# Expert results of a routed layer: plain scatters and two loads against adding scatters and one load

## The chip, the cores and the metric

One core of one Trainium2 chip runs the whole program. The metric is the device time of one execution in microseconds (us), the median of three runs.

## The reference, cut to what matters

Two layers work on 16 x 256 = 4096 tokens of 128 features, in fp32. Each layer has a mixing part (a scan in the first, an attention with relative positions in the second) and a feed-forward part with 8 experts, of which each token uses two. The change touches only the second layer's feed-forward part and what follows it:

```python
logits = relu(x @ Wr1 + br1) @ Wr2 + br2          # 8 experts
p = softmax(logits); (p1, e1), (p2, e2) = top_2(p)
w1, w2 = softmax over the pair, temperature 2      # b_ex = exp((p2 - p1) / 2), w1 = 1/(1 + b_ex), w2 = b_ex/(1 + b_ex)
shared = silu(x @ Ws1 + bs1) @ Ws2 + bs2
expert[e](x) = silu(x @ We1[e] + be1[e]) @ We2[e] + be2[e]
out = X + gate * (shared + w1 * expert[e1](x) + w2 * expert[e2](x))
```

The pair's weights are written here as the kernel computes them; x is the normed and modulated row of a token, X the residual row, gate a vector for each batch entry.

## The kernel before, in words

Tokens lie in 8 chunks of 512 (4 rows of each of 128 partitions, TPC = 4). The block after the attention is written out by hand for each engine. Routing goes in four groups of two chunks: `choose(g)` (lines 1493 to 1513, VectorE) finds the two experts of a token, `destinations(g)` (1515 to 1525) the two slots, and GpSimd scatters each token's row twice, with 64 indirect DMAs (line 741), into `dispatched_rows`, an area in DRAM where each expert has its rows together. A row is 128 features and one number, the place where the result has to go (RW = D + 1). Rows that no token fills come from a padding table that SP (SyncE) copied there early (lines 468 to 479).

Then 39 tiles (NG) of 256 rows run, each of one expert. Tile j uses slot k = j mod 4 of the buffers (UT = 4). The order of the queues for one tile is:

- SP, `next_tiles` (620 to 628): waits until tile j - 4 has left the slot (`s_ys`), loads the 256 rows (line 598) and the expert's weights, 578 KB (line 604).
- TensorE, in the order `up_tile(j)` (2142 to 2151), `transpose_tile(j + 1)` (2135 to 2140), `down_tile(j - 1)` (2153 to 2161).
- ScalarE, `hidden` (984 to 990): four Silu activations.
- VectorE, `tile_in(j + 1)` then `results(j - 1)` (1607 to 1620). `tile_in` waits for the transposes and for `s_yo[k]`, the landing of tile j - 4's scatters, because it overwrites their index column `rid` (line 1613); it then copies the transposed rows (1615). `results` adds the bias into `YS` (1619) and increments `s_ys`.
- GpSimd, `results_out` (745 to 751): waits for `s_ys` only, then issues two indirect DMAs (line 749), each 128 rows of 128 floats, to `expert_results`, where each token has two rows, one for each of its experts. Their landing is counted in `s_yo[k]`. Scatters of different tiles never meet in a row and may be under way together.

The end (the tail): once all scatters have landed SP loads both rows of every token, 16 loads of 256 KB (line 634). For each chunk ScalarE scales the first row by w1 (1004), VectorE adds w2 times the second (1645) and adds the gated sum into X (`add_gated`, lines 1127 and 1130), and SP stores the chunk (639). The weights of all tokens are worked out once, by VectorE and ScalarE (1598 to 1605, 982).

`link(...)` makes VectorE wait for its own instruction before the next one that reads its result.

Of the kernel before, what the change touches and what calls it, by code (L numbers as in the profile page):

```python
# [23 lines left out]
P = 128  # L24
# [11 lines left out]
E = 8  # L36
# [26 lines left out]
RW = D + 1  # L63
# [7 lines left out]
PADR = (E + SPARE) * GT  # L71


def build(nc, A, out):
    ctx = ExitStack()
    with ctx:
# [149 lines left out]
        rowid = R.take(2 * NT).rearrange("p (k t) -> p k t", k=2)  # L226
# [16 lines left out]
        b_m1, b_m2, b_w1, b_w2 = [R.take(NT) for _ in range(4)]  # L243
# [10 lines left out]
        YG = [v.rearrange("p t n -> p (t n)")[:, 0:NT * D].rearrange("p (t n) -> p t n", t=NT) for v in ROWS]  # L254
# [25 lines left out]
        yD = scratch("expert_results", [2 * TOK + PADR, D])  # L280
# [108 lines left out]
        s_xt = sem("s_xt")  # L389
        s_ys = sem("s_ys")  # L390
# [3 lines left out]
        s_y1 = sem("s_y1")  # L394
        s_fin = sem("s_fin")

# [34 lines left out]
        def _(sp):  # L431
# [149 lines left out]
            for dst, src in ((Wr1[:, :], A["wr1"]), (Wr2[0:33, :], A["wr2"]), (br1[0:32, :], A["br1"]),  # L581
                             (iota1[:, :], A["iota"]), (rowid[:, :, :], A["rowid"]), (steps[:, :, :], A["steps"]),
                             (below[:, :], A["below"]), (restart[:, :], A["restart"]), (reach[:, :, :], A["reach"]),
                             (woT1[:, :], A["woT1"]), (W1S[:, :], A["w1s"])):
                sp.dma_start(dst, src).then_inc(s_wm[1], 16)
# [46 lines left out]
            for c in range(NC):  # L632
                for k in range(2):
                    sp.dma_start(YG[k][:, c * TPC:(c + 1) * TPC, :],
                                 yD[k * TOK:(k + 1) * TOK, :].rearrange("(p t) d -> p t d", p=P)
                                 [:, c * TPC:(c + 1) * TPC, :]).then_inc(s_yl[c], 16)
            for c in range(NC):
                sp.wait_ge(s_fin, c + 1)
                sp.dma_start(out[c * CH:(c + 1) * CH, :].rearrange("(t p) d -> p t d", p=P),
                             X[:, c * TPC:(c + 1) * TPC, :]).then_inc(s_out, 16)  # L640
# [4 lines left out]
        def _(pool):  # L645
# [86 lines left out]
            pool.wait_ge(s_pad, 16 * (E + 1))  # L732
# [20 lines left out]
            with pool.Fori(0, FULL) as i:  # L753
                for k in range(UT):
                    results_out(i * UT + k, k)
            for k in range(LAST):
                results_out(FULL * UT + k, k)
# [3 lines left out]
        def _(act):  # L761
# [188 lines left out]
            values_out(NP - 1, (0, 1))  # L950
            features(3)
# [10 lines left out]
            rows_out(4)  # L962
            relative_out(NP - 1, (1, 2))
# [7 lines left out]
            for c in range(3):  # L971
                shared_hidden(c)
# [6 lines left out]
            for c in range(4, NC):  # L979
                shared_hidden(c)  # L980
            act.wait_ge(s_lg, GROUPS + 2)
            nc.scalar.activation(b_w2[:, :], b_m2[:, :], ACT.Exp).then_inc(s_el, 1)
# [16 lines left out]
            act.wait_ge(s_lg, GROUPS + 3)  # L999
            for c in range(NC):  # L1000
                act.wait_ge(s_yl[c], 32)
                for t in range(TPC):
                    T = c * TPC + t
                    ins = nc.scalar.activation(YG[0][:, T, :], YG[0][:, T, :], ACT.Copy, scale=b_w1[:, T:T + 1])
                ins.then_inc(s_y1, 1)
# [3 lines left out]
        def _(dve):  # L1009
# [424 lines left out]
            def ids(lo, hi):  # L1434
                for k in range(2):
                    ins = v.tensor_copy(ROWS[k][:, lo:hi, D:RW], rowid[:, k, lo:hi].unsqueeze(2))
                ins.then_inc(s_ids, 1)
# [55 lines left out]
            def choose(g):  # L1493
# [13 lines left out]
                link(best_of(b_CD[:, :, :], b_m2[:, ts], b_OH2[:, :, :]))  # L1507
                link(v.tensor_tensor(ME[:, :, :].rearrange("p e t -> p t e"), b_OH1[:, :, :], b_OH2[:, :, :], ALU.add))
# [89 lines left out]
            link(v.tensor_tensor(b_m2[:, :], b_m2[:, :], b_m1[:, :], ALU.subtract))  # L1598
            v.tensor_scalar(b_m2[:, :], b_m2[:, :], 0.5, None, ALU.mult).then_inc(s_lg, 1)
            for c in range(4, NC):  # L1600
                shared_out(c)
            dve.wait_ge(s_el, GROUPS + 2)
            link(v.tensor_scalar(b_w1[:, :], b_w2[:, :], 1.0, None, ALU.add))
            link(v.reciprocal(b_w1[:, :], b_w1[:, :]))
            v.tensor_tensor(b_w2[:, :], b_w2[:, :], b_w1[:, :], ALU.mult).then_inc(s_lg, 1)

            def tile_in(j, k):
# [5 lines left out]
                v.tensor_copy(rid[:, k, :].unsqueeze(2), XR[:, k, :, D:RW])  # L1613
# [27 lines left out]
            for c in range(NC):  # L1641
# [545 lines left out]
def constants():  # L2187
# [6 lines left out]
    k["rowid"] = np.stack([place, place + np.float32(TOK)], axis=1)  # L2194
    count = np.arange(64, dtype=np.float32)
    k["steps"] = np.tile(np.stack([count, count * np.float32(GT)])[None], (P, 1, 1))
    k["padding"] = np.zeros((PADR, RW), dtype=np.float32)
    k["padding"][:, D] = 2 * TOK + np.arange(PADR)
# [98 lines left out]
```

## Time and profile of the kernel before

| what | value |
|---|---|
| median of 3 runs | 961.08 us (956.97 to 962.22) |
| the profiled execution, first to last instruction | 1008.9 us |
| TensorE busy in it | 838.6 us (83%) |
| VectorE / ScalarE / GpSimd busy | 592.7 / 371.3 / 255.6 us |
| DMA | 108.37 MB, mean 107 GB/s |
| mean granted TensorE clock | 0.890 |

All durations below are from the profiled execution. The profile gives its span, 1008.9 us, and no other time of it; that is 47.8 us above the median of the unprofiled runs. In its rows a time is in us from the span's start; PE is TensorE, PEld its weight loads, DVE is VectorE, ACT ScalarE, POOL GpSimd, SP SyncE and SPq what SyncE's queue issues; "out<-in" names what an instruction writes and reads. A number in brackets behind a row is how long the engine had been idle before it, and behind the arrow stands what ended that.

### The profile page before, as it was taken

To read this page: it belongs to the slowest core of one execution; us is meant where nothing else is said; L and a number is where in the kernel's file an instruction comes from. 1 tells how busy PE (TensorE), PEld (TensorE's weight loads), DVE (VectorE), ACT (ScalarE), POOL (GpSimd) and SP (SyncE) were. 2 spreads that over 40 slices of the span, in tenths; PEclk is the share of its full clock that TensorE was granted. 3 is DMA by queue.
4 is the path that set the end of the run, shared out by engine and by line. 5 is a ranking of instruction groups with operands and counts; after the bars stand their busy time and mean duration, and the time that the engine had idled before them with its cause. 6 is when DMAs were issued, how large, how long until landed. Compare 5 with 4: busy or idle time off the path is not lost.

```text
span 1008.9 us, 22593 instructions
## 1 busy us (share of the span) xinstructions
PE 838.6 (83%) x8710; PEld 572.5 (57%) x8710; DVE 592.7 (59%) x1638; ACT 371.3 (37%) x719; POOL 255.6 (25%) x252
## 2 busy tenths in 40 slices
PE   5545698999958789999999999986679789999960
PEld 3443365656634446656656656553257578888850
DVE  8632866666688787687687687763245232222217
ACT  3335221222214105435435436553325324444424
POOL 0522000000073601012011112034661514444440
PEclk9956699999989958999999999997688779999985
DMA  5600022226414761133233332121310417777746
GB/s 147 268 3 0 1 92 92 92 92 211 140 49 140 233 174 48 29 95 89 46 94 60 74 94 62 31 59 34 86 41 9 131 55 213 212 220 215 212 130 223
DMA packets 107827, 108.37 MB, mean 107 GB/s; under 512 B 48892, under 2 KB 93644, under 8 KB 106796
## 3 DMA queue, kind: packets, MB, share of 16 engines
q1 hardware_dynamic: 103196, 97.82, 33.7%
q0 software_dynamic: 4544, 9.35, 2.6%
q8 instruction: 60, 0.98, 0.4%
q14 instruction: 27, 0.22, 0.1%
HBM read 82.15 MB, written 44.78 MB: 126 GB/s over the span
## 4 chain that ended last, share of the span: by engine, by line
PE 62%; DVE 18%; issue 7%; ACT 5%; POOL 3%; DMA 3%; SPq 2%; POOLq 0%; DVEq 0%; ACTq 0%
PE bank L2148 8%; PE bank L2158 7%; PE bank L1928 7%; PE bank L1762 5%; PE bank L1773 5%; PE bank L1774 4%; PE bank L1868 4%; DVE sb_arena L1360 4%; PE bank L2077 3%; PE bank L1820 3%; PE bank L2067 3%; PE bank L1846 3%; DVE sb_ST L1023 2%; DVE sb_arena L1350 2%; DVE sb_arena L1352 2%
## 5 line engine op out<-in xcount | busy, mean ns | idle before, releaser
L1360 DVE TRANSPOSE_TENSOR_REDUCE sb_arena<-bank 128x16 f32<-128x512 f32 x192 | 120.3, 685 | 25.4 <-PE bank L1868 24.2
L901 ACT ACTIVATE sb_arena<-bank 128x512 f32<-128x512 f32 x192 | 99.2, 602 | 50.0 <-PE bank L1868 50.0
L989 ACT ACTIVATE sb_arena<-bank,sb_arena 128x256 f32<-128x256 f32 x156 | 65.3, 471 | 99.9 <-PE bank L2148 99.1
L749 POOL DMA_INDIRECT expert_results<-sb_arena x78 | 74.7, 958 | 105.5 <-DVE sb_arena L1619 88.9
L1762 PEld LDWEIGHTS bank<-sb_arena 128*128 128x128 f32 x512 | 67.9, 195 | 42.1 <-issue 25.3
L858 ACT ACTIVATE sb_arena<-bank 128x512 f32<-128x512 f32 x64 | 38.2, 597 | 143.9 <-PE bank L1774 143.8
L2148 PE MATMUL bank<-sb_arena 128*128 128x256 f32 x312 | 80.3, 402 | 3.8 <-DVE sb_arena L1615 1.8
L1928 PE MATMUL bank<-sb_arena 128*16 128x128 f32 x1024 | 71.9, 422 | 9.5 <-issue 9.4
L1762 PE MATMUL bank<-sb_arena 128*128 128x128 f32 x512 | 70.2, 281 | 10.5 <-DVE sb_arena L1192 10.5
L741 POOL DMA_INDIRECT dispatched_rows<-sb_arena x64 | 63.0, 984 | 62.7 <-DVE sb_arena L1525 44.4
L2158 PE MATMUL bank<-sb_arena 128*128 128x128 f32 x624 | 75.9, 275 | 0.0
L1254 DVE SCALAR_TENSOR_TENSOR sb_arena<-bank,sb_arena 128x128 f32<-128x128 f32 x256 | 71.7, 343 | 2.0 <-PE bank L1762 2.0
L2158 PEld LDWEIGHTS bank<-sb_arena 128*128 128x128 f32 x624 | 72.8, 192 | 0.1
L1192 DVE TENSOR_TENSOR sb_arena<-sb_arena,bank 128x512 f32<-128x512 f32 x64 | 43.7, 685 | 49.6 <-ACT sb_arena L858 49.0
L1773 PE MATMUL bank<-sb_arena 128*128 128x512 f32 x128 | 69.0, 622 | 0.0
L1774 PE MATMUL bank<-sb_arena 128*128 128x512 f32 x128 | 67.5, 609 | 0.0
L2148 PEld LDWEIGHTS bank<-sb_arena 128*128 128x128 f32 x312 | 58.3, 197 | 15.5 <-issue 5.3
L1820 PE MATMUL bank<-sb_arena 128*128 128x56 bf16 (+1 forms) x512 | 62.2, 281 | 5.5 <-DVE sb_arena L1340 3.2
L1350 DVE CAST sb_arena<-bank 128x512 bf16<-128x512 f32 x64 | 43.7, 682 | 37.0 <-PE bank L1820 37.0
L1613 DVE CAST sb_arena<-sb_arena 128x2 uint32<-128x2 f32 x39 | 7.8, 200 | 97.9 <-DMA expert_results<-sb_arena 81.3
L1868 PE MATMUL bank<-sb_arena,sb_identb 128*32 128x128 bf16 (+1 forms) x2304 | 63.1, 242 | 0.4 <-DVE sb_arena L1350 0.4
L1846 PE MATMUL bank<-sb_arena 32*128 32x256 bf16 x512 | 52.9, 285 | 6.8 <-DVE sb_arena L1360 4.5
(263 smaller groups left out, 1356.5 us busy)
## 6 DMA issues: line engine op xcount, KB each, us to landing
sb_arena<-in_w SPq DMA_DIRECT2D x39, 578.0 KB
dispatched_rows<-in_padding SPq DMA_DIRECT2D x8, 2064.0 KB, 9.5
sb_arena<-dispatched_rows SPq DMA_DIRECT2D x39, 129.0 KB
sb_arena<-q_parts SPq DMA_DIRECT2D x8, 512.0 KB, 5.5
sb_arena<-k_parts SPq DMA_DIRECT2D x8, 512.0 KB, 7.0
context_rel<-sb_arena SPq DMA_DIRECT2D x256, 8.0 KB
sb_arena<-expert_results SPq DMA_DIRECT2D x16, 256.0 KB, 5.9
q_parts<-sb_arena SPq DMA_DIRECT2D x24, 128.0 KB, 2.4
```

Of the source, the lines that this page charges most:

```text
L749: nc.gpsimd.indirect_dma_start(yD[:, :], bass.IndirectOffsetOnAxis(ap=rid[:, k, r:r + 1], axis=0), YS[:, k, r, :], None).then_inc(s_yo[k], 16)
L901: nc.scalar.activation(dst, src, ACT.Exp).then_inc(s_ex, 1)
L1360: v.tensor_reduce(dst.rearrange("p h b -> p (h b)"), bank[r % RING][:, :].rearrange("p (b c) -> p b c", c=32), AX, ALU.max, apply_transpos ...
L1762: ins = mm(bank[4 + j % 2][:, t * D:(t + 1) * D], HM0[:, j % 2, t * P:(t + 1) * P], W0[:, k, 2 * F0:3 * F0], start=True, stop=True)
L1773: mm(bank[j % 2][:, :], W0[:, k, 0:F0], chunk(hT, c), start=True, stop=True)
L1774: mm(bank[2 + j % 2][:, :], W0[:, k, F0:2 * F0], chunk(hT, c), start=True, stop=True).then_inc(s_up[0], 1)
L1820: ins = mm(out[:, :, :, x], GT4[:, first:first + 32, :].rearrange("p x a -> p (x a)"), queries[:, :, :, q], start=True, stop=True, skip_gr ...
L1846: mm(dst[:, x * S:(x + 1) * S], KG[k][rows, g, 0:P], QG[k][rows, g, :], start=(x == 0), stop=False, skip_group_check=True)
L1868: ins = mm(dst[32 * b:32 * b + 32, :, 32 * b:32 * b + w], identb[:, 32 * a:32 * a + 32], src[:, :, :].rearrange("p (g b) q -> p g b q", g= ...
L1928: ins = mm(out[32 * j:32 * j + 2 * HD, :, x], relk[:, 32 * j + 8 * w + 2 * x:32 * j + 8 * w + 2 * x + 2, :], four, start=True, stop=True, ...
L2148: ins = mm(bank[2 * (k % 2) + b // 2][:, b % 2 * GT:(b % 2 + 1) * GT], W1[:, k, b * P:(b + 1) * P], XT[:, k % 2, :], start=True, stop=True ...
L2158: ins = mm(bank[6 + k % 2][:, r * D:(r + 1) * D], HMT[:, k % 2, b, r * P:(r + 1) * P], W1[:, k, I1 + b * D:I1 + (b + 1) * D], start=(b == ...
```

## The change

A dispatched row now carries its routing weight as well (RW = D + 2). VectorE works the pair's weights out group by group inside `choose` and `destinations`, with one exponential by ScalarE for each group (`pair_shares`). In the loop VectorE multiplies each result row by its weight, a second instruction in `results`. The scatters add into `expert_sums`, one row for each token, that SP fills with zeros early in the program. Two tiles may now add into the same token's row, so `results_out` waits, before it issues a tile's two scatters, until both scatters of the tile before it have landed. The tail loads one row for each token (8 loads), VectorE multiplies by the gate and adds into X for six chunks, and GpSimd does the same for chunks 2 and 6.

```diff
-RW = D + 1
+RW = D + 2
...
-        yD = scratch("expert_results", [2 * TOK + PADR, D])
+        zD = scratch("expert_sums", [TOK + GT, D])
...
+        BY_POOL, BY_DVE = (2, 6), (0, 1, 3, 4, 5, 7)
...
             sp.dma_start(xsD[AREA:, :], A["padding"][E * GT:, :]).then_inc(s_pad, 16)
+            sp.dma_start(zD[:, :], A["zeros"]).then_inc(s_pad, 16)
...
             for c in range(NC):
-                for k in range(2):
-                    sp.dma_start(YG[k][:, c * TPC:(c + 1) * TPC, :],
-                                 yD[k * TOK:(k + 1) * TOK, :].rearrange("(p t) d -> p t d", p=P)
-                                 [:, c * TPC:(c + 1) * TPC, :]).then_inc(s_yl[c], 16)
+                sp.dma_start(ZG[:, c * TPC:(c + 1) * TPC, :],
+                             zD[0:TOK, :].rearrange("(p t) d -> p t d", p=P)[:, c * TPC:(c + 1) * TPC, :]
+                             ).then_inc(s_yl[c], 16)
...
-            def results_out(j, k):
+            def results_out(j, k, before):
                 pool.wait_ge(s_ys, j + 1)
+                if before is not None:
+                    pool.wait_ge(s_yo[(k - 1) % UT], before)
                 pool.sem_inc(s_turn, 1)
                 for r in range(2):
                     nc.gpsimd.indirect_dma_start(
-                        yD[:, :], bass.IndirectOffsetOnAxis(ap=rid[:, k, r:r + 1], axis=0),
-                        YS[:, k, r, :], None).then_inc(s_yo[k], 16)
+                        zD[:, :], bass.IndirectOffsetOnAxis(ap=rid[:, k, r:r + 1], axis=0),
+                        YS[:, k, r, :], None, compute_op=ALU.add).then_inc(s_yo[k], 16)
...
+            for n, c in enumerate(BY_POOL):
+                pool.wait_ge(s_res, NC)
+                pool.wait_ge(s_yl[c], 16)
+                z4 = ZG[:, c * TPC:(c + 1) * TPC, :].rearrange("p (b t) f -> p b t f", b=2)
+                gate = GATE[:, 1, 2 * c:2 * c + 2, :].unsqueeze(2).to_broadcast([P, 2, 2, D])
+                nc.gpsimd.tensor_tensor(z4, z4, gate, ALU.mult).then_inc(s_gp, 1)
+                pool.wait_ge(s_gp, n + 1)
+                xs = X[:, c * TPC:(c + 1) * TPC, :]
+                nc.gpsimd.tensor_tensor(xs, xs, ZG[:, c * TPC:(c + 1) * TPC, :], ALU.add).then_inc(s_finp, 1)
...
+            def pair_shares(g):
+                act.wait_ge(s_df, g + 1)
+                nc.scalar.activation(b_ex[:, :], b_df[:, :], ACT.Exp, scale=0.5).then_inc(s_wx, 1)
...
             values_out(NP - 1, (0, 1))
+            pair_shares(0)
             features(3)
...
             shares(2)
-            for c in range(3):
+            shared_hidden(0)
+            pair_shares(2)
+            for c in range(1, 3):
                 shared_hidden(c)
...
             def destinations(g):
                 ts = slice(g * GN, (g + 1) * GN)
+                dve.wait_ge(s_wx, g + 1)
+                link(v.tensor_scalar(pairw[:, :], b_ex[:, :], 1.0, None, ALU.add))
+                link(v.reciprocal(pairw[:, :], pairw[:, :]))
+                v.tensor_copy(ROWS[0][:, ts, D + 1:RW], pairw[:, :].unsqueeze(2))
+                v.tensor_tensor(ROWS[1][:, ts, D + 1:RW], b_ex[:, :].unsqueeze(2), pairw[:, :].unsqueeze(2), ALU.mult)
                 dve.wait_ge(s_rank, g + 1)
...
             def results(j, k):
                 dve.wait_ge(s_dn[1], j + 1)
                 v.tensor_tensor(YS[:, k, :, :], bank[6 + k % 2][:, 0:GT].rearrange("p (r n) -> p r n", r=2),
-                                W1[:, k, OB:OB + D].unsqueeze(1).to_broadcast([P, 2, D]), ALU.add).then_inc(s_ys, 1)
+                                W1[:, k, OB:OB + D].unsqueeze(1).to_broadcast([P, 2, D]), ALU.add).then_inc(s_yb, 1)
+                dve.wait_ge(s_yb, j + 1)
+                v.tensor_tensor(YS[:, k, :, :], YS[:, k, :, :], XR[:, k, :, D + 1:RW].to_broadcast([P, 2, D]), ALU.mult
+                                ).then_inc(s_ys, 1)
...
-            for c in range(NC):
-                dve.wait_ge(s_y1, c + 1)
-                dve.wait_ge(s_yl[c], 32)
-                for T in range(c * TPC, (c + 1) * TPC):
-                    ins = v.scalar_tensor_tensor(out=YG[0][:, T, :], in0=YG[1][:, T, :], scalar=b_w2[:, T:T + 1],
-                                                 in1=YG[0][:, T, :], op0=ALU.mult, op1=ALU.add)
-                link(ins)
-                add_gated(c, YG[0][:, c * TPC:(c + 1) * TPC, :].rearrange("p (b t) f -> p b t f", b=2), 1, s_fin)
+            for c in BY_DVE:
+                dve.wait_ge(s_yl[c], 16)
+                z4 = ZG[:, c * TPC:(c + 1) * TPC, :].rearrange("p (b t) f -> p b t f", b=2)
+                gate = GATE[:, 1, 2 * c:2 * c + 2, :].unsqueeze(2).to_broadcast([P, 2, 2, D])
+                link(v.tensor_tensor(z4, z4, gate, ALU.mult))
+                xs = X[:, c * TPC:(c + 1) * TPC, :]
+                v.tensor_tensor(xs, xs, ZG[:, c * TPC:(c + 1) * TPC, :], ALU.add).then_inc(s_fin, 1)
```

The two ops that worked out all weights at once on ScalarE and VectorE (lines 982 and 1598 to 1605) and the scaling in the tail (lines 1004 and 1645) are gone. `pair_shares(1)` stands behind `rows_out(4)`, `pair_shares(3)` behind `shared_hidden(4)`.

## Rows read from the trace of the kernel before

**Rows 1.** Busy time of engines in stretches: PE, PEld, DVE, ACT, POOL, clock, DMA share, GB/s.

```profile
860.00:965.00 105.00, 103.75 (x693) 93.76 (x692) 25.35 (x80) 44.13 (x106) 51.32 (x54) 1.00 0.74 216
...
640.00:650.00 10.00, 8.28 (x181) 5.46 (x177) 6.70 (x21) 6.38 (x11) 0.00 (x0) 1.00 0.18 39
160.00:170.00 10.00, 7.32 (x24) 4.08 (x23) 5.92 (x19) 1.58 (x3) 0.00 (x0) 0.83 0.63 231
```

**Rows 2.** The chain that ended last, one tile of the loop (start, us, what).

```profile
861.87 1.99 PE bank L2148 x8
863.86 0.22 PE bank L2139 x2
864.08 1.79 PE bank L2158 x16
```

**Rows 3.** The same chain, from the last scatter to the end.

```profile
978.07 2.23 DMA expert_results<-sb_arena
980.44 0.34 SPq L634
980.83 3.21 DMA sb_arena<-expert_results
984.12 1.29 ACT sb_arena L1004 x4
...
985.51 1.15 DVE sb_arena L1645 x4
986.68 0.77 DVE sb_TMP L1127 x2
...
1005.49 0.69 DVE sb_X L1130
```

**Rows 4.** GpSimd in order of time, the loop's first scatters and its last.

```profile
827.48 0.95 POOL L749 DMA_INDIRECT expert_results<-sb_arena  x1 [28.63 <-DVE sb_arena L1619]
828.74 0.96 POOL L749 DMA_INDIRECT expert_results<-sb_arena  x1 [0.30 <-issue]
...
976.81 0.95 POOL L749 DMA_INDIRECT expert_results<-sb_arena  x1 [0.30 <-issue]
```

**Rows 5.** VectorE in order of time around the first scatters.

```profile
826.25 0.42 DVE L1619 TENSOR_TENSOR sb_arena<-bank,sb_arena 128x256 f32<-128x256 f32 x1 [1.29 <-PE bank L2158]
...
833.03 0.17 DVE L1613 CAST sb_arena<-sb_arena 128x2 uint32<-128x2 f32 x1 [2.33 <-DMA expert_results<-sb_arena]
```

**Rows 6.** Waits of the loop: who waited for whom, us in total, times, longest.

```profile
DVE sb_arena L1613 <- DMA expert_results<-sb_arena: 81.3, 33, 3.0
```

**Rows 7.** SyncE's queue in the loop, and the chain's first load of rows.

```profile
828.75 0.34 SPq L604 DMA_DIRECT2D sb_arena<-in_w  x1
...
811.92 2.22 DMA sb_arena<-dispatched_rows
```

**Rows 8.** DMA queue of the indirect DMAs (page, part 3): packets, MB, share.

```profile
q0 software_dynamic: 4544, 9.35, 2.6%
```

**Rows 9.** ScalarE and GpSimd in order of time: tables, tail, elementwise.

```profile
665.64 1.02 ACT L920 ACTIVATE sb_arena<-bank,sb_MOD 128x256 f32<-128x256 f32 x2
...
710.83 1.28 ACT L944 ACT_TABLE_LOAD   x1
...
994.13 2.60 ACT L1004 ACTIVATE sb_arena<-sb_arena 128x128 f32<-128x128 f32 x8 [0.54 <-DMA sb_arena<-expert_results]
...
665.86 1.27 POOL L710 TENSOR_TENSOR sb_arena<-sb_arena 128x512 f32<-128x512 f32 x1
```

**Rows 10.** VectorE in order of time: first group's weights would stand here.

```profile
669.06 0.28 DVE L1508 TENSOR_TENSOR sb_arena<-sb_arena 128x64 f32<-128x64 f32 x1
...
813.55 0.35 DVE L1604 RECIPROCAL sb_arena<-sb_arena 128x32 f32<-128x32 f32 x1
```

**Rows 11.** The chain of the loop's first tile, at the lower clock.

```profile
815.52 3.78 PE bank L2148 x8
819.30 0.44 PE bank L2139 x2
```

More of the change, by code:

```diff
@@ L225, in build @@
         iota1 = R.take(E)
-        rowid = R.take(2 * NT).rearrange("p (k t) -> p k t", k=2)
+        rowid = R.take(NT)
+        pairw = R.take(GN)
         steps = R.take(2 * 64).rearrange("p (k n) -> p k n", k=2)
@@ L242, in build @@
         texpu, tbaseu = [R.take(NG).bitcast(U32) for _ in range(2)]
-        b_m1, b_m2, b_w1, b_w2 = [R.take(NT) for _ in range(4)]
+        b_m1, b_m2 = [R.take(NT) for _ in range(2)]
+        b_df, b_ex = [R.take(GN) for _ in range(2)]
         R = Region(TOK)
@@ L253, in build @@
         ROWS = [v.rearrange("p (t n) -> p t n", t=NT) for v in (rows0, R.take(NT * RW))]
-        YG = [v.rearrange("p t n -> p (t n)")[:, 0:NT * D].rearrange("p (t n) -> p t n", t=NT) for v in ROWS]
+        ZG = ROWS[0].rearrange("p t n -> p (t n)")[:, 0:NT * D].rearrange("p (t n) -> p t n", t=NT)
         R = Region(pt_at)
@@ L393, in build @@
         s_turn = sem("s_turn")
-        s_y1 = sem("s_y1")
+        s_df = sem("s_df")
+        s_wx = sem("s_wx")
+        s_gp = sem("s_gp")
+        s_finp = sem("s_finp")
         s_fin = sem("s_fin")
+        BY_POOL, BY_DVE = (2, 6), (0, 1, 3, 4, 5, 7)
         block = ctx.enter_context(nc.Block())
@@ L632, in _ @@
             for c in range(NC):
-                for k in range(2):
-                    sp.dma_start(YG[k][:, c * TPC:(c + 1) * TPC, :],
-                                 yD[k * TOK:(k + 1) * TOK, :].rearrange("(p t) d -> p t d", p=P)
-                                 [:, c * TPC:(c + 1) * TPC, :]).then_inc(s_yl[c], 16)
+                sp.dma_start(ZG[:, c * TPC:(c + 1) * TPC, :],
+                             zD[0:TOK, :].rearrange("(p t) d -> p t d", p=P)[:, c * TPC:(c + 1) * TPC, :]
+                             ).then_inc(s_yl[c], 16)
             for c in range(NC):
-                sp.wait_ge(s_fin, c + 1)
+                if c in BY_POOL:
+                    sp.wait_ge(s_finp, 1 + BY_POOL.index(c))
+                else:
+                    sp.wait_ge(s_fin, 1 + BY_DVE.index(c))
                 sp.dma_start(out[c * CH:(c + 1) * CH, :].rearrange("(t p) d -> p t d", p=P),
@@ L749, in results_out @@
                     nc.gpsimd.indirect_dma_start(
-                        yD[:, :], bass.IndirectOffsetOnAxis(ap=rid[:, k, r:r + 1], axis=0),
-                        YS[:, k, r, :], None).then_inc(s_yo[k], 16)
-            with pool.Fori(0, FULL) as i:
+                        zD[:, :], bass.IndirectOffsetOnAxis(ap=rid[:, k, r:r + 1], axis=0),
+                        YS[:, k, r, :], None, compute_op=ALU.add).then_inc(s_yo[k], 16)
+            for k in range(UT):
+                results_out(k, k, 32 if k else None)
+            with pool.Fori(1, FULL) as i:
                 for k in range(UT):
-                    results_out(i * UT + k, k)
+                    results_out(i * UT + k, k, 32 * i + (32 if k else 0))
             for k in range(LAST):
-                results_out(FULL * UT + k, k)
+                results_out(FULL * UT + k, k, 32 * (FULL + 1) if k else 32 * FULL)
+            for n, c in enumerate(BY_POOL):
[7 more added lines that the diff above has]
+                nc.gpsimd.tensor_tensor(xs, xs, ZG[:, c * TPC:(c + 1) * TPC, :], ALU.add).then_inc(s_finp, 1)
         @block.scalar
@@ L962, in _ @@
             rows_out(4)
+            pair_shares(1)
             relative_out(NP - 1, (1, 2))
@@ L978, in _ @@
             shares(3)
-            for c in range(4, NC):
+            shared_hidden(4)
+            pair_shares(3)
+            for c in range(5, NC):
                 shared_hidden(c)
-            act.wait_ge(s_lg, GROUPS + 2)
-            nc.scalar.activation(b_w2[:, :], b_m2[:, :], ACT.Exp).then_inc(s_el, 1)
             def hidden(j, k):
@@ L998, in _ @@
                 hidden(FULL * UT + k, k)
-            act.wait_ge(s_lg, GROUPS + 3)
-            for c in range(NC):
[L1001 to L1005, printed above, removed]
         @block.vector
@@ L2193, in constants @@
     place = (np.arange(P)[:, None] * NT + np.arange(NT)[None, :]).astype(np.float32)
-    k["rowid"] = np.stack([place, place + np.float32(TOK)], axis=1)
+    k["rowid"] = place
     count = np.arange(64, dtype=np.float32)
     k["steps"] = np.tile(np.stack([count, count * np.float32(GT)])[None], (P, 1, 1))
-    k["padding"] = np.zeros((PADR, RW), dtype=np.float32)
-    k["padding"][:, D] = 2 * TOK + np.arange(PADR)
+    k["padding"] = np.zeros((PADR, GT, RW), dtype=np.float32)
+    k["padding"][:, :, D] = TOK + np.arange(GT)
+    k["padding"] = k["padding"].reshape(PADR * GT, RW)
+    k["zeros"] = np.zeros((TOK + GT, D), dtype=np.float32)
     k["restart"] = np.tile((np.arange(GE) % GN != 0).astype(np.float32), (P, 1))
```

19 lines of the change are left out of this document (7 added, 12 removed).

## The prediction

> **What bounds the kernel now.** I read the busy table of the expert loop first. In a stretch of 105 us TensorE is busy for 103.75, at the full granted clock (1.00, so 2.4 GHz), while the DMA engines stand at 0.74 [rows 1]. The chain of work that ended last says the same for one tile: four blocks up, two transposes and the down products of the tile before follow each other without a gap, 1.99 + 0.22 + 1.79 = 4.00 us [rows 2]. So the loop is TensorE's. GpSimd needs 0.96 + 0.30 + 0.95 us for a tile's two scatters and issues them 1.26 us apart [rows 4]; it sits idle for the rest, and no tile waits until another's scatters have landed, except at one place. VectorE's index copy (line 1613) waits for the landing of tile j - 4: 33 times, 81.3 us in all [rows 6]. That costs TensorE nothing yet, but it tells how long a scatter takes. Behind the loop the chain turns to the tail: last scatter 978.07 to 980.30, then loads, ScalarE's scaling and VectorE's eight chunks, the last instruction ending at 1006.18 [rows 3], and the last store up to 1008.9. From the last landing to the end that is 28.6 us.
>
> **The tail: a saving.** The first load is issued 0.14 us after the last landing and has arrived at 984.04 [rows 3], 3.74 after it; that stays. ScalarE's 1.29 us for the first chunk goes [rows 3]. VectorE needs 1006.18 - 985.51 = 20.67 us for eight chunks, 2.58 each [rows 3]; the four multiply-adds (1.14) go, and what is left is a product and a sum over 128x512. The sum is 0.69 [rows 3]; the product is as large, so 0.69 + 0.69 + 0.07 for the link = 1.45, and six chunks are 8.7 us. Can the loads keep up? Now 16 of them are in by about 994 (ScalarE's last wait for one ends at 994.13 [rows 9]), so each after the first costs about (994.1 - 984.0)/15 = 0.67 us; eight are in at 3.74 + 4.7 = 8.4 us after the landing, and VectorE's last chunk begins about 11. GpSimd's two chunks are two instructions of 1.27 each at this size [rows 9] and end before that. The new tail is 3.74 + 8.7 + 2.7 (last sum to the end, 1006.18 to 1008.9) = 15.2 us, a saving of 13.4.
>
> **Ahead of the loop: small.** The zeros are 2.2 MB, issued by SP before a long wait, and nobody needs them before the loop's first scatter at 827.48 [rows 4]; nothing, or 10 us at 216 GB/s [rows 1] were that cover gone. In each of four groups VectorE gets five instructions on 128x8 that take between 0.17 and the 0.35 of the reciprocal on 128x32 [rows 10], some 1.2 us with links, in a stretch where it mostly waits for TensorE. ScalarE gets four exponentials. The first blocks its queue: `pair_shares(0)` needs a difference that VectorE has just before 669.06, and `features(3)`, behind it, now starts at 665.64 [rows 9, 10]: up to 3.4 us late, of which an idle stretch of TensorE later may take up all. The third stands between two Silu blocks and brings two table loads of 1.28 [rows 9]. Bounds: 0 and 11 (four times 1.2, 3.4, 2.6). I take 2, near the lower end, since TensorE waits for other things in that stretch. In the loop the second instruction in `results` costs VectorE 0.42 (as its neighbour on the same shape [rows 5]) + 0.03 each tile; VectorE is 24% busy [rows 1]; only the first one, 0.45, lies on the path.
>
> **The loop: a new wait.** GpSimd now waits, before each tile's scatters, until the tile before has landed. Behind that wait nothing else is queued on GpSimd but the scatters, yet VectorE's `tile_in` waits for their landing, TensorE's `up_tile` waits for `tile_in`, and SP's loads wait for `results`: four slots are the only slack, and a queue that is slower than TensorE uses them up in a few tiles. So the scatters' own round becomes a candidate for the period: wake, first issue, second issue, landing.
> - Wake: `results` ends at 826.25 + 0.42 = 826.67 and the scatter starts at 827.48: 0.81 [rows 4, 5]. The lower bound is 0.30, the gap when nothing is waited for [rows 4].
> - First to second issue: 1.26 [rows 4].
> - Second issue to landing: alone, 2.23 (978.07 to 980.30) [rows 3]. With the weights' load issued beside it at 828.75 [rows 7], VectorE is let go at 833.03, 828.74 + 4.29 [rows 4, 5].
> - The add itself: no row has an adding DMA. It has to read the destination, so it costs between nothing and a whole read of DRAM behind the write, 2.22 for the nearest load [rows 7]. I take half, 1.1, since the issue is shared and the read can't be.
>
> I take the landing alone: in the new steady state a tile's `results` comes about 1.6 us after a landing (index copy, row copy, bias, product), SP issues the weights 828.75 - 826.67 = 2.08 later [rows 5, 7], so 3.7 after it, while the second scatter goes out at 0.81 + 1.26 = 2.1. The weights mostly come behind it. The period is then 0.81 + 1.26 + 2.23 + 1.1 = 5.40 us against TensorE's 4.00: the loop is GpSimd's, and TensorE idles for a quarter of it.
>
> **The sum.** First scatter 827.48 + 0.45 = 827.93; 38 periods, 205.2; the last tile's 1.26 + 2.23 + 1.1 = 4.6: last landing 1037.7 instead of 980.3, +57.4. Tail -13.4, ahead of the loop +2: +46.0, a span of 1054.9. With P for the period the change is 39 P - 164.6: it is zero at 4.22, and half a per cent (4.8 us, about what a measurement of this kernel can tell from no change) is reached at 4.10 and 4.34. The median of the runs shown is 47.8 us below the profiled span; I can't see where, so I carry the difference over as it is: 961.08 + 46 = 1007. Scaled with 961/1009 it would be 1005.
>
> **Rivals.**
> - TensorE stays the bound, faster. If GpSimd wakes after 0.30 and the add is free, P = 0.30 + 1.26 + 2.23 = 3.79, below TensorE's 4.00; what remains is -13.4 + 2 + 0.45 = -11: 950. Against it: every wait for another engine in rows 4 and 5 costs 0.81. It decides at P = 4.10. Chance 0.08; another 0.07 for a P of 4.10 to 4.34, where tail and loop cancel.
> - The add costs only traffic. The 142 indirect DMAs took 2.6% of 16 engines' span [rows 8], 1008.9 x 0.026 / 142 = 0.18 us each; once more of it for the read gives P = 4.48, +10: 971. Chance 0.13.
> - Contention: weights and scatter meet as now, P = 0.81 + 1.26 + 4.29 = 6.36, or 7.46 with the add's 1.1: 1045 to 1087. For it: 81.3 us of VectorE's waits [rows 6] show that this landing is the usual one today. Against it: the phase worked out above. Chance 0.15 beyond P = 6.5, together with an add slower than a whole read.
> - The clock falls. With a quarter of each tile idle TensorE might be granted 1.2 GHz; a tile would take 3.78 + 0.44 + 2 x 1.79 = 7.8 us [rows 2, 11], and 39 x 7.8 gives 1100. A stretch busy for 0.73 shows a clock of 0.83, one busy for 0.83 shows 1.00 [rows 1]; and at half the clock TensorE would have no gaps left. Chance 0.02.
> - That the wait does nothing is excluded: each value it waits for is that of the tile just before.
>
> A rule that speaks against the change, in sentences of its own. The Trainium skill, "DMA: Bandwidth & Descriptors", section "Anatomy of one DMA", puts nearly all of a GpSimd DMA's fixed time of 2.0 us into the receipt of the last write, so a wait for it buys no transfer, only latency; with its fit an estimate for 64 KB is 2.15, which would make P 4.22 without the add, a change of nothing, and the trace's 2.23 agrees. The Trainium skill, "Collectives: The Full Stack", section on the bandwidth ceiling, says that a DMA's add costs no cycles, only a second source read on the same ring; by that rule the traffic rival is right and the time is about 971, and no run here shows it yet.
>
> **Chances and range.** The forecast holds for P from 4.6 to 6.5, 976 to 1050, with 0.55. Slower 0.55 + 0.13 + 0.15 + 0.02 = 0.85, same 0.07, faster 0.08. The range reaches from P = 4.25, 962, which leaves 0.13 below it, to P = 6.97, 1068, which leaves 0.07 above.
>
> **What would show it.** In the profile after: TensorE busy for about 0.75 of the loop, still at clock 1.00; GpSimd's scatter in pairs 1.26 apart that start 5.4 us after each other, the idle time before each first one ended by a DMA and not by VectorE; from the last landing to the end about 15 us. Pairs 4.0 apart, or gaps ended by VectorE, prove the first rival; 4.5 the second; above 6.3, with the weights' issue just before the second scatter, the third; an `up` block of 3.8 us the clock. A scatter instruction much longer than 0.96 would mean that the add costs GpSimd and not the DMA.

## The result and the profile after

The kernel after takes 1093.26 us (median of 4, 1089.62 to 1096.18), the kernel before 961.65 us beside it: ratio 1.138, 95% interval 1.134 to 1.142. It is 132 us slower; I had said 46 slower, with a range that ended at 1068.

The kernel before took 957 to 963 us in this comparison and, on the three chips of the later ones, 994 to 1023 (one run of 17 on one of them apart, 1200), and each version is compared only with the kernel before beside it. The profile shown ahead (span 1008.9) is of the longer kind, the profile after (span 1090.3) of the shorter one. Up to about 680 us the two profiles agree within what the views show; the dispatch stretch behind it makes the difference, and the loop's first scatter stands at 779.85 in the profile after and at 827.48 in [rows 4]. The period of the loop (from one tile's first scatter to the next tile's) and the tail agree within 0.2 us in the two profiles of the kernel after, one of each kind.

GpSimd in order of time, kernel after: two neighbouring tiles in the middle of the loop, then the last two (start, us, engine, line, what; in brackets the idle time before, and what ended it).

```profile
927.09 1.56 POOL L762 DMA_INDIRECT expert_sums<-sb_arena  x1 [4.28 <-issue]
928.95 1.55 POOL L762 DMA_INDIRECT expert_sums<-sb_arena  x1 [0.30 <-issue]
934.82 1.56 POOL L762 DMA_INDIRECT expert_sums<-sb_arena  x1 [4.32 <-DMA expert_sums<-sb_arena]
...
1060.87 1.56 POOL L762 DMA_INDIRECT expert_sums<-sb_arena  x1 [2.45 <-issue]
1062.73 1.55 POOL L762 DMA_INDIRECT expert_sums<-sb_arena  x1 [0.30 <-issue]
1066.70 1.56 POOL L762 DMA_INDIRECT expert_sums<-sb_arena  x1 [2.41 <-issue]
1068.57 1.56 POOL L762 DMA_INDIRECT expert_sums<-sb_arena  x1 [0.31 <-issue]
```

In the brackets "issue" means that the view names nothing that was waited for; those gaps are as long as the one that it puts down to a DMA (4.28 and 4.32 us), so I read them as the same wait. Beside [rows 4] three things are new. A scatter instruction takes 1.56 us instead of 0.96, so the pair is 1.86 apart instead of 1.26. The next pair starts 5.87 us after the second scatter while the loop loads weights (928.95 to 934.82), and 3.97 after it in the last four tiles, for which no weights are loaded any more (1062.73 to 1066.70). The period is 7.7 us in the loop and 5.8 at its end; over all 38 it is (1066.70 - 779.85) / 38 = 7.55, where TensorE's was about 4.0.

SyncE's queue and VectorE around the same tiles show what meets what.

```profile
929.92 0.35 SPq L613 DMA_DIRECT2D sb_arena<-in_w  x1
...
926.42 0.17 DVE L1639 CAST sb_arena<-sb_arena 128x2 uint32<-128x2 f32 x1 [6.46 <-DMA expert_sums<-sb_arena]
...
934.13 0.17 DVE L1639 CAST sb_arena<-sb_arena 128x2 uint32<-128x2 f32 x1 [6.38 <-DMA expert_sums<-sb_arena]
```

VectorE is let go by a landing at 926.42 and again at 934.13. Between them the second scatter starts 2.5 us after the landing, its instruction ends at 930.50, and the weights go out at 929.92: 0.97 us behind its start and 0.58 ahead of its end.

The waits of the loop, kernel after (who waited for whom: us in total, times, longest), and busy times of the stretch that [rows 1] shows for before:

```profile
DVE sb_arena L1639 <- DMA expert_sums<-sb_arena: 217.5, 34, 7.2
ACT sb_arena L1022 <- PE bank L2176: 205.7, 52, 7.3
PE bank L2176 <- DVE sb_arena L1641: 92.3, 33, 4.1
...
860.00:965.00 105.00, 67.44 (x353) 58.07 (x352) 16.74 (x52) 21.94 (x53) 40.76 (x27) 0.85 0.49 113
```

VectorE's wait for landings has grown from 81.3 us [rows 6] to 217.5, and TensorE now waits for VectorE. TensorE is busy for 0.64 of the stretch instead of 0.99, and the DMA share has fallen from 0.74 to 0.49: neither is used up; the loop waits for a round trip. The tail, in the chain that ended last:

```profile
1068.57 3.25 DMA expert_sums<-sb_arena
...
1071.96 3.04 DMA sb_arena<-expert_sums
...
1075.10 0.70 DVE sb_arena L1674
...
1078.62 1.68 DVE sb_arena L1674
1080.30 0.02 issue
1080.32 1.63 DVE sb_X L1676
...
1086.31 0.69 DVE sb_X L1676
```

The last landing is at 1071.82, the end at 1090.3: 18.5 us instead of 28.6. Some of VectorE's instructions take 0.69 us and some 1.46 to 1.75, all of one shape. Its six chunks take 1075.10 to 1087.00 = 11.9 us.

The balance: first scatter to last landing 1071.82 - 779.85 = 292.0 instead of 980.30 - 827.48 = 152.8, +139.2; the tail -10.1; together +129, and 132 is what was measured.

### The profile page after: what moved, and what is told of

Read it like the earlier page. It is cut to its first block and busy times, and to the rows that moved or that the text cites. A ratio compares the mean times of both kernels' runs of the same rounds, so it can differ in the third digit from the quotient of the medians.

```text
span 1090.3 us, 22577 instructions
## 1 busy us (share of the span) xinstructions
PE 857.3 (79%) x8710; PEld 589.7 (54%) x8710; DVE 599.9 (55%) x1648; ACT 362.9 (33%) x692; POOL 308.4 (28%) x256
## 5 line engine op out<-in xcount | busy, mean ns | idle before, releaser
L2176 PE MATMUL bank<-sb_arena 128*128 128x256 f32 x312 | 107.4, 504 | 94.7 <-DVE sb_arena L1641 94.7
L762 POOL DMA_INDIRECT expert_sums<-sb_arena x78 | 121.5, 1558 | 187.0 <-issue 98.5
L2176 PEld LDWEIGHTS bank<-sb_arena 128*128 128x128 f32 x312 | 74.2, 249 | 114.5 <-issue 93.8
L1790 PEld LDWEIGHTS bank<-sb_arena 128*128 128x128 f32 x512 | 67.8, 195 | 42.2 <-issue 25.4
L2186 PE MATMUL bank<-sb_arena 128*128 128x128 f32 x624 | 82.6, 290 | 0.0
L2186 PEld LDWEIGHTS bank<-sb_arena 128*128 128x128 f32 x624 | 80.8, 209 | 0.1
L1790 PE MATMUL bank<-sb_arena 128*128 128x128 f32 x512 | 70.2, 281 | 10.5 <-DVE sb_arena L1218 10.5
L1956 PE MATMUL bank<-sb_arena 128*16 128x128 f32 x1024 | 68.0, 423 | 1.3 <-ACT sb_arena L903 1.3
L686 POOL TENSOR_TENSOR sb_TMP<-sb_arena,sb_GATE 128x256 f32<-128x256 f32 x16 | 11.3, 726 | 186.5 <-DVE sb_arena L1280 186.4
```

The costliest lines, as they stand in the source:

```text
L762: nc.gpsimd.indirect_dma_start(zD[:, :], bass.IndirectOffsetOnAxis(ap=rid[:, k, r:r + 1], axis=0), YS[:, k, r, :], None, compute_op=ALU.ad ...
L1790: ins = mm(bank[4 + j % 2][:, t * D:(t + 1) * D], HM0[:, j % 2, t * P:(t + 1) * P], W0[:, k, 2 * F0:3 * F0], start=True, stop=True)
L1956: ins = mm(out[32 * j:32 * j + 2 * HD, :, x], relk[:, 32 * j + 8 * w + 2 * x:32 * j + 8 * w + 2 * x + 2, :], four, start=True, stop=True, ...
L2176: ins = mm(bank[2 * (k % 2) + b // 2][:, b % 2 * GT:(b % 2 + 1) * GT], W1[:, k, b * P:(b + 1) * P], XT[:, k % 2, :], start=True, stop=True ...
L2186: ins = mm(bank[6 + k % 2][:, r * D:(r + 1) * D], HMT[:, k % 2, b, r * P:(r + 1) * P], W1[:, k, I1 + b * D:I1 + (b + 1) * D], start=(b == ...
```

## The experiments

Line numbers are those of each kernel's own profile.

**The kernel before again.** No edit.

> The kernel before, profiled once more. The profiled span shown ahead was 1008.9 us, 47.8 above the median of the unprofiled runs, and the kernel after has its first scatter of the loop at 779.9 instead of 827.5. Theory 1 (those 48 us are stalls of that one execution, between 680 and 811): a new profile has its first scatter of expert results near 780 and a span near 960. Theory 2 (the change made the stretch before the loop shorter, and profiling costs this kernel 48 us): the span is near 1009 again, the first scatter near 827.

1014.5 us, beside 1016 for the kernel before in the same comparison; span 1012.7, first scatter of the loop at 830.04. Theory 1 as I wrote it (a flaw of one execution) is wrong, theory 2 (profiling costs 48 us) as well, since the unprofiled runs here take as long as the profile. What is left is a difference between the places the program runs in, the same for profiled and other runs; no run shows where it comes from.

**The wait alone.**

```diff
-            def results_out(j, k):
+            def results_out(j, k, before):
                 pool.wait_ge(s_ys, j + 1)
+                if before is not None:
+                    pool.wait_ge(s_yo[(k - 1) % UT], before)
...
```

> The kernel before with one part of the change alone: GpSimd waits for the landing of the tile before, the scatters stay plain and go to two rows for each token. Theory round trip: the period of the loop is wake 0.7 + first to second issue 1.26 + landing 2.23 + what the weights' load in flight adds. If the second scatter gets out ahead of the weights, 4.2 to 4.5 us, and the time is 970 to 985. Theory contention as it stands in the kernel after: another 1.9, 6.1 us, about 1040. Theory that the add's own throughput is what costs: the wait alone costs nothing, about 961.

1041.02 us, ratio 1.028 (1.019 to 1.036) to the kernel before: +25, just above the 9 to 24 that my 970 to 985 stood for. The first three periods are 6.06, 5.36 and 4.86, from the fourth on they are 4.3 to 4.5 but for one of 6.65. GpSimd, SyncE and VectorE, two tiles:

```profile
900.10 0.96 POOL L751 DMA_INDIRECT expert_results<-sb_arena  x1 [2.04 <-issue]
901.36 0.95 POOL L751 DMA_INDIRECT expert_results<-sb_arena  x1 [0.30 <-issue]
904.54 0.95 POOL L751 DMA_INDIRECT expert_results<-sb_arena  x1 [2.22 <-issue]
...
902.81 0.06 SPq L604 DMA_DIRECT2D sb_arena<-in_w  x1
...
903.86 0.17 DVE L1617 CAST sb_arena<-sb_arena 128x2 uint32<-128x2 f32 x1 [3.56 <-DMA expert_results<-sb_arena]
```

From the second scatter to the next tile's first: 3.18 us, of which 2.50 are the landing, as VectorE sees it (903.86), and 0.68 the wake. Alone it was 2.23 [rows 3]. The weights go out 1.45 us after the second scatter and 0.5 after its instruction ended. So for a plain scatter the phase (when in a tile's round the weights go out, against the second scatter) is what I had worked out: the weights come behind it, and in steady state the period is 0.35 us above 4.00. Over the whole loop the wait costs more: from the first tile's scatter to the last tile's 170.6 us instead of 149.3 [rows 4], 0.56 a tile, with the slow start and the one period of 6.65 in it.

That one period shows within one kernel what the phase does. There the second scatter started 0.6 us late, and the weights went out 0.35 us behind its start, 0.62 before its instruction ended:

```profile
945.58 0.97 POOL L751 DMA_INDIRECT expert_results<-sb_arena  x1 [0.92 <-issue]
945.93 0.35 SPq L604 DMA_DIRECT2D sb_arena<-in_w  x1
949.59 0.17 DVE L1617 CAST sb_arena<-sb_arena 128x2 uint32<-128x2 f32 x1 [5.70 <-DMA expert_results<-sb_arena]
```

VectorE was let go 4.01 us after that scatter's start, against 2.25 to 2.57 in the other tiles from the fourth on, whose weights went out 0.80 to 1.47 behind it. In the kernel of waits with plain scatters below the same tile's second scatter started as late, its weights went out 1.23 behind it, and the landing took 2.29.

**The add alone**, into rows of its own, no wait.

```diff
+                sp.dma_start(yD[n * TOK:n * TOK + rows, :], A["zeros"][0:rows, :]).then_inc(s_pad, 16)
...
-                        YS[:, k, r, :], None).then_inc(s_yo[k], 16)
+                        YS[:, k, r, :], None, compute_op=ALU.add).then_inc(s_yo[k], 16)
```

> The kernel before with the other part alone: the scatters add, into rows of their own (two for each token, filled with zeros early, 6.2 MB), and no tile waits for another. Theory round trip: the add matters only because somebody waits for it; GpSimd needs 1.86 x 2 = 3.7 us for a tile, under TensorE's 4.0, so the loop stays within 3% and the time is 961 to 975. Theory that adding DMAs are slow as such (their packets take 3.7 times as long): the loop stays at 7.7 us for a tile and the time is 1100.

1020.41 us, ratio 1.010 (1.001 to 1.020): +4. First to last scatter of the loop 155.4 us (825.54 to 980.9) instead of 150.6, with an average period of 4.04 instead of 3.93. Its busy times in the stretch of [rows 1]:

```profile
860.00:965.00 105.00, 102.04 (x684) 92.68 (x682) 24.90 (x80) 43.62 (x104) 81.39 (x53) 1.00 0.96 213
```

TensorE is still busy for 0.97 at the full clock, but GpSimd is now at 0.78 and the DMA engines at 0.96 instead of 0.74. The adding scatter alone hardly slows the loop, though GpSimd and the DMA engines have little room left.

**Both, and nothing else of the change.** The two edits above together.

> The kernel before with both parts, the wait and the add, but nothing else of the change: no weight in the rows, no second instruction on VectorE, the tail as before, two rows for each token. The wait alone gave a period of 4.35 us, the add alone 4.0. Theory that the two multiply each other (the add lengthens exactly the round that the wait exposes, and so makes it meet the weights' load): 7.5 to 7.8 us for a tile, about 140 us above the kernel before on the same chip. Rival, that the rest of the change has its part: 5.5 to 6.5.

1159.6 us (one run; the kernel before beside it 994 to 1021), periods 6.9 to 8.7, 5.8 to 6.0 in the last four. From the first tile's scatter to the last tile's it takes 1123.32 - 834.93 = 288.4 us, the kernel after 1066.70 - 779.85 = 286.9, the kernel before 149.3. Alone the wait adds 21 us to this and the add 4, together they add 139. So the two parts make the whole loss of the loop; weights in the rows, VectorE's second instruction and the new tail have no part in it that shows.

**The waits with plain scatters**, the rest as in the kernel after.

```diff
-                        YS[:, k, r, :], None, compute_op=ALU.add).then_inc(s_yo[k], 16)
+                        YS[:, k, r, :], None).then_inc(s_yo[k], 16)
```

> The kernel after with its waits, but the scatters overwrite the token's row instead of adding to it, so that the output lacks one of the two experts' parts. Theory round trip: as for the wait alone, 4.2 to 4.5 us for a tile if the weights come behind the second scatter, 6.1 if they meet; total about 950 to 965, or 1030. If the add costs nothing, 7.7 us and 1093 as measured.

Periods 4.5 to 4.9 in steady state, 1029.8 us (one run). The period is 0.3 above that of the wait alone; the weights leave 1.5 us after the second scatter here too, and I haven't pursued it. The time came out above both of my ranges since those were taken from a kernel before of 961; against 1016 beside it, it is +13.

**The kernel after again**, on the same chip as the next three.

> The kernel after once more, beside the kernel before on the same chip. The kernel before took 961 us in the first comparison and 1016 in the second; its dispatch stretch is 47 us longer in the slow profiles. If that is a property of the place the program runs in, both kernels show it, and the difference stays at 130 us (139 in the loop, -10 in the tail), whatever the level. If the change had removed it, the difference shrinks to 80 us where the kernel before takes 1010.

1142.72 us, ratio 1.131 (1.126 to 1.136) to a kernel before of 1011: +132, as in the first comparison. Its first scatter stands at 829.25, where [rows 4] has 827.48. So the change does nothing to the stretch ahead of the loop that I can tell from the spread there (825.5 to 836.5 in all profiles but the first one after), and the place moves both kernels alike.

**Few weights.** From tile 4 on the loop loads 16 columns of the weights.

```diff
-                load_weights(j, k)
+                e = sp.value_load(texpu[0:1, bass.ds(j, 1)], min_val=0, max_val=E - 1)
+                sp.dma_start(W1[:, k, 0:16], A["w1"][bass.ds(e, 1), :, 0:16].rearrange("o p n -> p (o n)")
+                             ).then_inc(s_ew[k], 16)
```

> The kernel after, but from tile 4 on the loop loads only 16 of 1156 columns of the expert's weights, so that the results of most tiles use the wrong weights; waits and order stay. Theory of the meeting weights (the adding scatter and the weights' load are under way together, which costs 1.9 us of the 7.7): the period is 5.8 to 5.9 from the start on, as in the last four tiles of the kernel after, and the time falls by about 33 x 1.9 = 63 us. Theory that the add is slow by itself while the loop runs (reads of rows, TensorE's phase): it stays at 7.7.

```profile
940.60 1.56 POOL L764 DMA_INDIRECT expert_sums<-sb_arena  x1 [2.54 <-issue]
942.47 1.55 POOL L764 DMA_INDIRECT expert_sums<-sb_arena  x1 [0.31 <-issue]
946.52 1.56 POOL L764 DMA_INDIRECT expert_sums<-sb_arena  x1 [2.50 <-issue]
```

5.8 to 6.1 us for a tile from the third on, but for two of 6.5, 4.05 from the second scatter to the next tile's first; 1084.2 us, 59 under the kernel after (one run). The meeting with the weights' load is 1.8 of the 7.7 us.

**Early weights.** SyncE waits for one more landing and so issues rows and weights just behind it.

```diff
                     sp.wait_ge(s_ys, i * UT - UT + k + 1)
+                    landed = 32 * i if k else 32 * i - 32
+                    if not isinstance(landed, int) or landed:
+                        sp.wait_ge(s_yo[(k - 1) % UT], landed)
...
```

> The kernel after, all computed as there, but SyncE also waits for a landing before it issues rows and weights, so that they go out right behind a landing, about 0.2 us after it, and not 2 to 3.5 us after it. Theory of the meeting weights: their 3.8 us to landing are over before the second adding scatter's data moves (4.1 us after the landing), the period falls to 5.9 to 6.3, the time by 50 to 65 us. Rival: what counts is the traffic in the period, not its phase, and it stays at 7.7.

1106.97 us, ratio 1.096 (1.091 to 1.101), 36 us under the kernel after on the same chip; the period is 6.4 to 6.9 in most tiles, 6.7 on average. GpSimd and SyncE:

```profile
1003.58 1.56 POOL L766 DMA_INDIRECT expert_sums<-sb_arena  x1 [3.24 <-issue]
1005.44 1.56 POOL L766 DMA_INDIRECT expert_sums<-sb_arena  x1 [0.31 <-issue]
1010.22 1.56 POOL L766 DMA_INDIRECT expert_sums<-sb_arena  x1 [3.22 <-issue]
...
1004.91 0.35 SPq L613 DMA_DIRECT2D sb_arena<-in_w  x1
```

The weights now go out 0.5 us ahead of the second scatter, and that scatter's round is 4.78 us instead of 5.87: with the same traffic, the phase decides over 1.1 of the 1.8 us. That the traffic alone counts is wrong; that this phase would free the scatter of the weights is wrong too, since I had expected 5.9 to 6.3. What the remaining 0.7 is wasn't taken apart. The opposite phase, weights held back until the adding scatter's instruction has ended, wasn't run; it would have been the direct test.

**The tail on VectorE alone.**

```diff
-        BY_POOL, BY_DVE = (2, 6), (0, 1, 3, 4, 5, 7)
+        BY_POOL, BY_DVE = (), tuple(range(NC))
```

> The kernel after with all eight chunks of the tail on VectorE and none on GpSimd. In the kernel after VectorE's instructions take 0.69 us alone and up to 1.68 while GpSimd works. Theory that the two engines slow each other down so much that the help brings nothing: VectorE's tail takes 8 x 1.4 = 11.2 us instead of 11.9, the end comes within 1 us of the kernel after, measured from the last landing (18.5 us). Theory that the help is real: the tail is 2 to 3 us longer.

Every one of the 16 instructions takes 0.68 or 0.69 us; the first starts at 1129.12 and the last ends at 1139.84, 10.7 us for eight chunks. From the last landing (1122.68 + 3.24 = 1125.92) to the end (1142.6) it is 16.7 us, against 18.3 in the repeated kernel after and 18.5 in the first. GpSimd's two chunks cost 1.6 to 1.8 us and save none.

**Two plain rows, weights in the rows.** The kernel after with the scatters, the rows and the missing wait of the kernel before; the tail sums two loads.

```diff
-                if before is not None:
-                    pool.wait_ge(s_yo[(k - 1) % UT], before)
...
-                        YS[:, k, r, :], None, compute_op=ALU.add).then_inc(s_yo[k], 16)
+                        YS[:, k, r, :], None).then_inc(s_yo[k], 16)
...
+                zs = ZG[:, c * TPC:(c + 1) * TPC, :]
+                link(v.tensor_tensor(zs, zs, YG[1][:, c * TPC:(c + 1) * TPC, :], ALU.add))
```

> A version that may beat both: rows carry their weight and VectorE multiplies in the loop, as in the kernel after, but the scatters stay plain, go to two rows for each token and wait for nothing, as in the kernel before; the tail loads both rows, and VectorE (six chunks) and GpSimd (chunks 2 and 5) each do sum, product with the gate, sum. The loop stays at 4.0 us for a tile; the tail is 3.7 + six chunks of 2.1 to 2.6 + 2.7 = 19 to 22 us instead of 28.6: 7 to 10 us faster than the kernel before. If GpSimd and VectorE slow each other down in the tail, 3 to 5.

1016.07 us, ratio 1.0065 (1.0028 to 1.0102) to 1011 beside it: 5 us slower, where I had expected 3 to 10 faster. From the first to the last scatter of the loop it needs 992.50 - 836.54 = 156.0 us, where [rows 4] have 978.07 - 827.48 = 150.6, and the tail is 25.1 instead of 28.6. So 5.4 us in the loop take the tail's saving. Of the edits left here VectorE's second instruction for each tile, which I had hidden beside TensorE, is the likely cause, but no run has it alone. One tile, and the waits between the loop's first and last scatter:

```profile
904.93 0.17 DVE L1641 CAST sb_arena<-sb_arena 128x2 uint32<-128x2 f32 x1 [3.24 <-DMA expert_results<-sb_arena]
...
PE bank L2180 <- DVE sb_arena L1643: 5.1, 8, 0.9
```

TensorE waited for VectorE's copy 8 times, 5.1 us in all (once, 0.6 us, in the kernel before), and before that copy VectorE had itself waited 3.24 us for a landing. So the second instruction wasn't in the copy's way there; I take it that a result 0.45 us later makes the scatters and their landing later, which isn't shown.

**The same, tail on VectorE alone.**

> The version with two plain rows for each token and weights carried in the rows, now with all eight chunks of the tail on VectorE. From the last load's issue order to the end 3.9 + 8 x 2.08 + 2.7 = 23.2 us instead of 24.9 with GpSimd's help and 28.5 in the kernel before; the loop's 5 us over the kernel before (VectorE's second instruction for each tile) stay. The time is equal to that of the kernel before within 0.5%, and 1 to 2 us under the version with GpSimd.

1017.15 us, ratio 1.014 (1.001 to 1.027), too wide to tell it from the version above. The tail is 1017.1 - 992.3 = 24.8 us, against the 23.2 expected: VectorE waited 1.47 us for the second chunk's load. The loop is 156.4. No version I ran beats the kernel before.

## Why the prediction was wrong

**Direction and the wait: right; what its landing meets: wrong.** The loop became GpSimd's, by the round of wake, two issues and landing, behind a wait that the slots couldn't absorb. The size was off: +46 forecast, +132 measured. By my own formula, 39 P - 164.6, the period P decides, and it was 5.40 in the forecast against 7.7 measured in steady state (7.55 over all tiles, which gives +130).

**Its terms, one by one.** The wake, 0.81: about 0.7 (1062.73 + 3.25 = 1065.98 to 1066.70). First to second issue, 1.26 from [rows 4]: 1.86. This is the term that I took from a plain scatter without asking whether the add changes the instruction; I had put all of the add behind the issue and named a longer instruction only as something that might be seen. The landing with the add, 2.23 + 1.1 = 3.33: 3.25 when alone. So "half a read" had the right size, a choice between two bounds; no run shows that a read is what it is. Contention, set to nothing: 1.9, a landing of 5.18 (928.95 to 934.13) against 3.25. Sum 0.7 + 1.86 + 3.25 + 1.9 = 7.7.

**The step that failed** is "the weights mostly come behind it". With it the contention term was set to nothing, and it is 1.9 of the 2.3 us that the period was off; the other term that was off by much is the two issues, 1.86 for 1.26. The argument held for a plain scatter, as the wait alone shows (4.35 a tile). It compared 3.7 us after the landing for the weights with 2.1 for the start of the second scatter. But two starts are the wrong thing to compare: in the one odd tile of the wait alone the weights went out 0.35 behind the plain scatter's start, and the landing took 4.01 all the same; from 0.80 behind it on they did no harm, in an instruction of 0.96. With the add the second instruction starts at 2.5 and ends at 4.1 after the landing, and the weights, issued at 3.5 (929.92 against 926.42), go out in between, 0.97 behind its start. With few weights the 1.8 us are gone, so it is the meeting that costs them. That weights issued behind the end of the adding scatter's instruction would do no harm is my reading and was not shown: no run sends them out there. I had the add's price in the sum and left it out of the phase.

**The range.** The contention rival with the add's 1.1 stood at P = 7.46 and 1087; the measured time is 6 us above it. It is as near as that in part by luck: its landing, 4.29 + 1.1 = 5.39, is 0.2 too long, its wake 0.1, and its two issues 0.6 too short. My sign for it, weights just before the second scatter, didn't come true either: they go out 0.97 behind its start. I gave everything beyond P = 6.5 a chance of 0.15 and cut the range inside it. The trace's most frequent landing [rows 5, 6] was the contended one, 4.29, and I set it aside on an estimate of phase that was made of terms I didn't know.

**The traffic rival** was wrong at 971. The add isn't free of its own cost: the queue's share in the profile after is

```profile
q0 software_dynamic: 13280, 9.38, 6.0%
```

for the same number of DMAs as [rows 8] and bytes that differ by 0.3%. Of 0.06 x 16 x 1090.3 = 1047 us the 64 plain scatters take 64 x 2.96 = 189, which leaves 11.0 us for each adding one, or 0.69 on each of 16 engines, 3.7 times the 0.18 of a plain one, in 144 packets instead of 32. This is the time of the packets, waits among them, and in the other kernels with adding scatters the same working gives 3.2 (both parts) to 4.2 times (the add alone). The Trainium skill, "Collectives: The Full Stack", section on the bandwidth ceiling, has the add in a reduce-scatter cost only its second source read, twice the traffic on the reading side. For this scatter the trace disagrees, with 3.7 times the engines' time and 0.6 us more in the instruction. The Trainium skill, "DMA: Bandwidth & Descriptors", section "Anatomy of one DMA", puts most of a GpSimd DMA's fixed time into its completion. That was the better guide: the DMA engines are idle for half of the loop (share 0.49) while it waits for landings, though no view here splits a landing into its parts.

**The other rivals.** TensorE stays the bound: no, the add alone shows it would without the wait. The clock: the granted clock in the loop's stretch is 0.85 instead of 1.00, and some tiles' up blocks run at the lower level (1.2 GHz), 3.78 us instead of 1.99, this one behind an idle gap of 3.71:

```profile
934.80 3.78 PE L2176 MATMUL bank<-sb_arena 128*128 128x256 f32 x8 [3.71 <-DVE sb_arena L1641]
```

It costs next to nothing, because TensorE is hardly waited for: VectorE's bias waits for it 4 times in this loop, 6.0 us in all, of 287. So a clock that falls came true as a sign and not as the cause.

**Tail and stretch ahead.** Forecast -13.4, measured -10.1. The missing 3.3 is in VectorE's six chunks, 11.9 us instead of 8.7. Without GpSimd's help eight chunks took 10.7, that is 8.0 for six, so the help made VectorE's six 3.9 us slower; giving it up gains only 1.6, since VectorE then has two chunks more. I had priced GpSimd's work and not what it does to VectorE. Ahead of the loop I had +2; nothing shows above the spread of the profiles. That these two sum to what was left of the gain was never decisive.

**The baseline.** I took the 47.8 us between span and median as a cost to carry over unchanged. They are the same for both kernels in absolute terms wherever both ran, and carrying the difference over was right: +132 both times.

## What to carry to other kernels

A wait on a DMA's landing turns its latency into a period, and the latency to put in is that of the changed DMA in its new phase: each term that an edit lengthens moves all later ones against the other traffic. Two edits that cost little alone (over the loop 0.56 us a tile for the wait, 0.11 for the add) cost 3.7 us a tile together, since the add lengthens the round that the wait exposes and moves it into the weights' load; test them together or work out the whole round with both. And where the trace's usual value of a price is the bad one, keep it inside the range however good the argument against it.

## What the runs showed of the hardware

- An indirect DMA that adds: instruction 1.56 us instead of 0.96, start to landing alone 3.25 instead of 2.23, 144 packets instead of 32 for 64 KB, and 3.2 to 4.2 times the DMA engines' time, by kernel.
- A 578 KB load lengthens the landing of a 64 KB scatter by where it is issued. Plain: 4.0 us with the load 0.35 us behind the scatter's start (one tile), 2.25 to 2.57 with it 0.80 to 1.47 behind. Adding: 5.2 with it 0.97 behind, 4.1 with it 0.5 ahead, 3.25 without it.
- VectorE and GpSimd slow each other down on fp32 sums and products in on-chip memory: 0.69 us alone, 1.46 to 1.75 beside GpSimd, whose own take 1.09 to 1.59 then. In the tail the help of GpSimd cost 1.6 us. The Trainium skill, "SBUF — State Buffer", section "SBUF: two separate sides", has the two engines arbitrate for one pair of ports that one instruction holds for its whole length. The trace agrees as far as it goes: the longer ones take 0.77 to 1.06 us more than VectorE's own 0.69, and the shortest of GpSimd's here takes 1.09. My tail sum had left that out. GpSimd, kernel after:

```profile
1076.67 1.40 POOL L779 TENSOR_TENSOR sb_arena<-sb_arena,sb_GATE 128x512 f32<-128x512 f32 x1 [6.55 <-DMA sb_arena<-expert_sums]
1078.15 1.59 POOL L782 TENSOR_TENSOR sb_X<-sb_X,sb_arena 128x512 f32<-128x512 f32 x1
```

- The stretch in which GpSimd's 64 dispatch scatters run took some 47 us more in all profiles but one (first scatter of the loop at 825 to 837 instead of 780), and the totals of both kernels with it. The cause is open; in the profile shown ahead engines idle there with no releaser named, or a remote one.
